# First mixing moved between the small tiles and the dense second convolution, with PSUM bank sets that swap at each step

## The reference, cut to what matters

```python
x = x + mix(x, cond, L0)      # 128x128 matrix and bias, mixed from 8 by an attention of the sample
x = x + conv(x, cond, L1)     # 9 taps over time, 4 groups of 32 channels, plus a bias of the sample
x = x + mix(x, cond, L2)
x = x + conv(x, cond, L3)
```

## Time and profile before

| | |
|---|---|
| median of 3 runs | 2650.08 us |
| the profiled execution, its own time | 2650.44 us |
| its span, first to last instruction | 2648.6 us |
| PE busy | 2627.4 us (99%) |
| PE weight loads busy | 1808.4 us (68%) |
| DVE busy | 2143.3 us (81%) |
| ACT busy | 2034.7 us (77%) |
| POOL busy | 818.0 us (31%) |
| granted TensorE clock, mean | 0.999 |

### The profile page before, as it was taken

The page is one execution under the profiler, slowest core; times in us unless marked ns, Lnnn a source line. Parts: engine busy times, 40 slices in busy tenths (PEclk is TensorE's granted clock), DMA queues, the critical chain, the costliest instruction groups (busy, mean ns, idle before and its releaser), DMA issues.

```text
span 2648.6 us, 106673 instructions
## 1 busy us (share of the span) xinstructions
PE 2627.4 (99%) x42610; PEld 1808.4 (68%) x42610; DVE 2143.3 (81%) x3093; ACT 2034.7 (77%) x3605; POOL 818.0 (31%) x1040
## 2 busy tenths in 40 slices
PE   9999999999999999999999999999999999999997
PEld 6667666766676667666766676667666766676665
DVE  8888788878887888788878887888788878887884
ACT  7777777777777777777777777777777777777774
POOL 1233233323332333233323332333233323332332
PEclk9999999999999999999999999999999999999999
DMA  4565556555655565556555655565556555655554
GB/s 166 182 205 185 180 184 195 187 180 184 196 187 180 184 195 187 180 183 196 187 180 183 194 189 180 183 195 188 180 183 195 188 180 183 195 189 180 182 176 149
DMA packets 228046, 489.82 MB, mean 185 GB/s; under 512 B 47016, under 2 KB 129072, under 8 KB 195376
## 3 DMA queue, kind: packets, MB, share of 16 engines
q1 hardware_dynamic: 228016, 489.39, 58.7%
HBM read 205.04 MB, written 150.99 MB: 134 GB/s over the span
## 4 chain that ended last, share of the span: by engine, by line
PE 98%; DVE 1%; ACT 0%; issue 0%; DVEq 0%; ACTq 0%
PE ps L361 42%; PE ps L342 28%; PE ps L313 14%; PE ps L326 13%; DVE y L680 0%; DVE y L674 0%; DVE xp L652 0%; DVE m_sum L632 0%; DVE prod L627 0%; PE ps L259 0%; DVE y_full L703 0%; PE ps L428 0%; PE ps L301 0%; PE ps L264 0%; DVE x_t L715 0%
## 5 line engine op out<-in xcount | busy, mean ns | idle before, releaser
L361 PE MATMUL ps<-y,conv_parts 32*128 32x512 f32 x18432 | 1141.7, 395 | 3.9 <-DVE y_full L703 1.8
L361 PEld LDWEIGHTS ps<-y,conv_parts 32*128 32x128 f32 x18432 | 906.5, 183 | 283.1 <-issue 131.4
L781 POOL COPY bias<-bias_table 128x4 f32 (+3 forms) x512 | 317.6, 621 | 1795.5 <-DMA o_ch<-o_ph 896.9
L680 DVE TENSOR_TENSOR y<-y_full,y 128x512 fp32r<-128x512 f32 x1020 | 636.6, 688 | 221.9 <-ACT y L497 221.9
L342 PE MATMUL ps<-y_full,conv_raw 32*32 32x512 f32 (+1 forms) x16384 | 753.8, 596 | 1.7 <-DVE y_full L703 1.7
L491 ACT ACTIVATE y_full<-ps,bias 128x512 f32<-128x512 f32 x1016 | 602.6, 707 | 26.6 <-issue 16.2
L546 ACT ACTIVATE o_ph<-ps,bias 128x512 f32<-128x512 f32 x508 | 308.5, 693 | 371.5 <-PE ps L361 371.5
L497 ACT CAST y<-y_full 128x512 fp32r<-128x512 f32 x1020 | 566.8, 663 | 0.7 <-DVE y_full L703 0.7
L342 PEld LDWEIGHTS ps<-y_full,conv_raw 32*32 32x32 f32 (+1 forms) x16384 | 275.5, 116 | 408.4 <-issue 406.2
L787 POOL COPY o_t<-o_ch 128x512 f32<-128x512 f32 x508 | 528.5, 1186 | 26.9 <-DMA o_ch<-o_ph 26.9
L491 ACT ACTIVATE y<-ps,bias 128x512 fp32r<-128x512 f32 x516 | 313.0, 690 | 191.3 <-PE ps L342 176.6
(11 more groups left out here) (60 smaller groups left out, 74.6 us busy)
## 6 DMA issues: line engine op xcount, KB each, us to landing
x_t<-x SPq DMA_DIRECT2D x128, 1024.0 KB, 5.0
o_ch<-o_ph SPq DMA_DIRECT2D x2032, 64.0 KB, 2.0
out<-o_t SPq DMA_DIRECT2D x127, 1024.0 KB, 4.0
m_parts<-mixed SPq DMA_DIRECT2D x512, 128.0 KB, 2.6
mixed<-m_own SPq DMA_DIRECT2D x128, 128.0 KB, 1.7
conv_raw<-conv_w SPq DMA_DIRECT2D x2, 768.0 KB, 9.8
mix_sb<-mix_w SPq DMA_DIRECT2D x2, 576.0 KB, 7.4
out<-x_t SPq DMA_DIRECT2D x4, 256.0 KB, 4.2
```

Source lines behind the costliest of these rows:

```text
L361: ins = nc.tensor.matmul(ps[:, bank + t, :], conv_parts[layer][rows, w, s - DENSE[0], :], src[rows, a, p_in, q:q + N], start=first, stop=f ...
L680: nc.vector.tensor_tensor(dst, full, high.bitcast(fp32), ALU.subtract).then_inc(low_set[layer], 1)
L781: nc.gpsimd.tensor_copy(bias[layer][:], bias_table[:, bass.ds(j, 1), COLUMN[layer]:COLUMN[layer] + WIDTH[layer]].rearrange("c j g -> c (j ...
```

## The change

The diff, cut to its core; left out are the bank argument that each helper now takes, the fold of the two `y1_full` buffers into one, and the written-out step 0.

```diff
+                if has(i, inner, 2):
+                    sp.wait_ge(in_time_set, 4 * (i - 1))
+                    sp.dma_start(out[i - 2], o_t[:]).then_inc(out_done, 16)
+                moves = has(i, inner, 1) and (inner or not is_last(i))
+                if moves:
+                    shuffle(i - 1, 0)
+                if has(i, inner, -1):
+                    store_matrix(i + 1)
+                if moves:
+                    for g in range(1, G):
+                        shuffle(i - 1, g)
+                if has(i, inner, -1):
+                    load_matrix(i + 1, False)
                 if has(i, inner, -3):
                     sp.wait_ge(x_low_set, 4 * (i + 2))
                     load_x(i + 3)
-                if has(i, inner, 2):
-                    sp.wait_ge(in_time_set, 4 * (i - 1))
-                    sp.dma_start(out[i - 2], o_t[:]).then_inc(out_done, 16)
-                if has(i, inner, -1):
-                    store_matrix(i + 1)
-                if has(i, inner, 1) and (inner or not is_last(i)):
-                    for g in range(G):
-                        shuffle(i - 1, g)
-                if has(i, inner, -1):
-                    load_matrix(i + 1, False)
...
-            def sparse(layer, src, begins, wait_bank):
-
-                bank = 4 if layer == 1 else 0
-                lots = WIDE + NARROW if begins else NARROW + WIDE
+            def sparse(layer, src, bank, lots):
+
...
-                        if r == 0 and begins:
-                            wait_bank(t)
                         for s, p, width in units:
                             q, p_in = divmod(s, PH)
-                            final = r == len(lots) - 1 and not begins
+                            final = layer == 1 and units is WIDE[-1]
                             if final:
                                 ins.then_inc(mm[1], 1)
...
                     q, p_in = divmod(s, PH)
+                    if k == len(order) - 1:
+                        wait_last()
                     for n, (w, a) in enumerate(PASSES):
                         first = k == 0 and n == 0 and begins
                         final = k == len(order) - 1 and n == len(PASSES) - 1 and not begins
+                own, other = own_banks(odd), other_banks(odd)
+
                 def free1(t):
-                    if not inner and i == B - 1:
-                        pe.wait_ge(full_set[2], 4 * i)
-                    elif inner or i > 0:
-                        pe.wait_ge(full_set[2], nth(i - 1, t))
+                    if inner or i > 1:
+                        pe.wait_ge(phases_set, nth(i - 2, t))
+                    elif i == 1:
+                        pe.wait_ge(full_set[0], nth(1, t))
                     elif t % 2 == 0:
                         pe.wait_ge(table_act, 2 - t // 2)
                     else:
                         pe.wait_ge(table_dve, 2 - t // 2)
 
-                def free3(t):
-                    if has(i, inner, -1):
-                        pe.wait_ge(full_set[0], nth(i + 1, t))
-                    else:
-                        pe.wait_ge(phases_set, nth(i - 2, t))
-
                 def free0(q):
                     if inner or i > 0:
-                        pe.wait_ge(phases_set, nth(i - 1, q))
+                        pe.wait_ge(low_set[1], nth(i, q))
                     else:
-                        pe.wait_ge(full_set[0], nth(1, q))
+                        pe.wait_ge(full_set[0], nth(0, q))
+
+                def free2(p):
+                    if has(i, inner, -1) and (inner or i > 0):
+                        pe.wait_ge(full_set[0], nth(i + 1, p))
+
+                def third_ready():
+                    if has(i, inner, 1):
+                        if not inner and i == 1:
+                            pe.wait_ge(conv_set, 2)
+                        pe.wait_ge(full_set[2], 4 * i)
 
                 if has(i, inner, 0):
                     if not inner and i == 0:
                         pe.wait_ge(zeros_set, 1)
                         pe.wait_ge(conv_set, 1)
                     pe.wait_ge(low_set[0], 4 * (i + 1))
-                    dense(1, y1, True, free1)
+                    dense(1, y1, own, free1, third_ready)
                     if not inner and i == 0:
                         side_bias()
                         pe.wait_ge(full_set[0], G)
-                    sparse(1, y1_full[odd], False, free1)
+                    sparse(1, y1_full, own, NARROW)
+                else:
+                    third_ready()
+                if has(i, inner, 1):
+                    sparse(3, y3_full, other, NARROW)
+                if has(i, inner, 0):
+                    sparse(1, y1_full, own, WIDE)
+                if has(i, inner, 1):
+                    sparse(3, y3_full, other, WIDE)
                 if not inner and i == 0:
                     pe.wait_ge(ctx_read, 2)
-                    first_mix(1, lambda q: pe.wait_ge(full_set[0], nth(0, q)))
+                    first_mix(1, 0, free0)
+                elif has(i, inner, -1):
+                    first_mix(i + 1, own, free0)
                 if has(i, inner, 1):
-                    if not inner and i == 1:
-                        pe.wait_ge(conv_set, 2)
-                    pe.wait_ge(full_set[2], 4 * i)
-                    sparse(3, y3_full, True, free3)
                     pe.wait_ge(low_set[2], 4 * i)
-                    dense(3, y3, False, free3)
+                    dense(3, y3, other, lambda t: None, lambda: None)
                 if has(i, inner, 0):
-                    second_mix(i)
-                if has(i, inner, -2):
-                    first_mix(i + 2, free0)
+                    second_mix(i, own, free2)
...
+                if has(i, inner, 0):
+                    high_1(i, own_banks(odd), False)
                 if has(i, inner, -1):
-                    full_0(i + 1, 1 - odd)
-                high_2(i - 1, not inner and i == 1)
+                    full_0(i + 1, own_banks(odd))
+                    high_0(i + 1)
+                output(i - 1, other_banks(odd), not inner and is_last(i), not inner and i == 1)
+                if has(i, inner, 0):
+                    full_2(i, own_banks(odd), False)
+                    high_2(i, False)
                 if has(i, inner, -2):
                     x_high(i + 2)
-                if has(i, inner, 0):
-                    high_1(i, False)
-                if has(i, inner, -1):
-                    high_0(i + 1, 1 - odd)
-                output(i - 1, not inner and is_last(i), not inner and i == 1)
-                if has(i, inner, 0):
-                    full_2(i, False)
...
+                if has(i, inner, 0):
+                    low_1(i, own_banks(odd))
                 if has(i, inner, -2):
                     matrix(0, i + 2)
+                if has(i, inner, -1):
+                    low_0(i + 1)
+                if has(i, inner, -2):
                     halves(0, i + 2)
-                low_2(i - 1)
-                if has(i, inner, -2):
-                    x_low(i + 2)
-                if has(i, inner, 0):
-                    low_1(i)
                 if has(i, inner, -1):
                     matrix(2, i + 1)
                     halves(2, i + 1)
-                    low_0(i + 1, 1 - odd)
-                if not inner and i in (B - 2, B - 1):
-                    full_2(i)
+                if has(i, inner, 0):
+                    if not inner and i == B - 1:
+                        full_2(i, own_banks(odd))
+                    low_2(i)
+                if has(i, inner, -2):
+                    x_low(i + 2)
...
-                if has(i, inner, 0) and (inner or i > 0):
-                    pool.wait_ge(full_set[2], 4 * i)
-                    set_bias(2, i)
                 if has(i, inner, 2):
                     if inner or i > 2:
                         pool.wait_ge(out_done, 16 * (i - 2))
                     for p in range(PH):
                         pool.wait_ge(shuffled[p], 16 * G * (i - 1))
-                if has(i, inner, -2):
-                    pool.wait_ge(full_set[0], 4 * (i + 2))
-                    set_bias(0, i + 2)
+                if has(i, inner, 0) and (inner or i > 0):
+                    pool.wait_ge(full_set[2], 4 * i)
+                    set_bias(2, i)
                 if has(i, inner, 2):
                     in_time(i - 2)
                 if has(i, inner, -1):
                     pool.wait_ge(low_set[1], 4 * (i + 1))
                     set_bias(1, i + 1)
+                if has(i, inner, -2):
+                    pool.wait_ge(full_set[0], 4 * (i + 2))
+                    set_bias(0, i + 2)
                 if has(i, inner, 0) and (inner or i > 0):
                     pool.wait_ge(phases_set, 4 * i)
                     set_bias(3, i)
```

(33 more changed lines are left out.)

57 lines of the change are left out of this document (34 added, 23 removed).

## The result

The changed kernel takes 2654.48 us (median of 20 runs, 2652.97 to 2657.73) against 2650.70 for the kernel before in the same series; the ratio is 1.0014, 95% interval 1.0008 to 1.0021, so it is slower by 3.8 us. The forecast was 2635.8. The profiled execution has a span of 2653.0 us where 2634.4 was worked out.

What follows compares the result with a forecast made beforehand. PE, busy for 99% of the span, was taken as the bound. Step 20.38 - 0.44 + 0.28 + 0.05 = 20.27; span 61.4 + 125 x 20.27 + 39.2 = 2634.4, time 2635.8 us, range 2594 to 2655.

Steps and rivals of the forecast that it cites:

- Bounds and seams: PE busy for 99% of the span; tile-shape seams per step fall from six to four, 1.28 to 0.84, saving 0.44 us.
- W to F: Closing from the 64-column rounds to F, a price with no row: excess taken as 0.19, between 0.13 and 0.32.
- the N rounds stand four in a row; I take 0.43: 32-column rounds on PE: the third and fourth cost 0.43 us each, W's steady round, rather than 0.45.
- both unseen prices: W to F's closing and the third and fourth N rounds; together they could shift the step by -0.06 to +0.18 us.
- D1's wait: D1's fourth product waits for ACT's output: 0.20 late plus 0.08 in the next round, +0.28 us a step, bounds 0 to 0.35.
- waking: PE starts 0.15 us after the work it waits for is ready, taken from a start at 56 us.
- F's wait: F(i+1) waits on DVE's low_1(i), nearly a tie behind W3: +0.05 us a step, between 0 and 0.2.
- a wait of 0.2 for the halves: SP's matrix store waits some 0.2 us for halves(2) between the first and second shuffle; said to cost nothing.
- Start: Written-out start: F(2) waits for low_1(1) until about 51 us; D1(2) at 61.4 us, an estimate to 2 us.
- rival D: Both waits at their upper ends, or W to F at 0.32: step 20.34 to 20.42, 2644 to 2655 us; chance 0.17.
- the likeliest case: The forecast's own case: a faster kernel, 2618 to 2645 us, chance 0.52.
- The three signs of a wrong forecast: Output ends before 2.9 after D3's last round; F starts over 2.5, or low_1 later than 1.4, after W1's last round.

Runs made afterwards that it cites:

- e2: Changed kernel, with ACT's output waiting for the bias and the four shuffles before the second convolution, not after; 2637.22 us, ratio 0.9958 to the kernel before.
- e7: Changed kernel, with SP's store of the mixed matrix behind all four shuffles instead of behind the first; 2652.19 us (one run).
- e1: Changed kernel, with the second convolution's 32-column lot put back behind the 64-column lots; 2641.88 us, ratio 0.997 to the kernel before.

## Why the prediction was wrong

- **Bounds and seams: right, but not the whole.** PE stays the bound, and F's new place gives 0.23 a step: before, F adds a closing and an opening on each side (0.13 + 0.10 + 0.09 + 0.10 = 0.42); between the small tiles and D3 it adds 0.19, its own opening 0.10 and the closing to D3 0.09, since the other two stand there anyway. M2 and D3 came out at 2.81 and 4.26 for 2.80 and 4.26. W to F, taken at 0.62, closes at 0.56, by the closer starts behind four N rounds. What is missing is a third price beside seams and new waits: PE's look-ahead ran out inside one shape.
- **The step that failed: "the N rounds stand four in a row; I take 0.43".** It was sized with the wrong question. I asked what a round costs and looked at W rounds, of which four are 64 instructions; of N rounds two are. So W's rounds at 0.43 could not tell what happens when two N lots follow, and the bounds of "-0.06 to +0.18" for both unseen prices together did not hold it: the four rounds cost 0.35 more, 0.30 with W's share, 38 us in 125 steps. The runs with 12 and 8 products and the doubled lot show why. Grouping the lots was to save one closing and one opening, 0.19 + 0.02 = 0.21; it lost 0.30.
- **D1's wait: right in kind and place, too large.** Forecast +0.28, measured 0.15 to 0.17 over a D1 without it (4.46 against 4.31 on average in e2, 4.29 in the step shown). The part that was mis-sized is waking: 0.15 was taken from a start at 56 us with PE idle; here the fourth product's weights load 0.05 after the output ends. Why waking is shorter here no run shows. The unhidden load, 0.08 forecast, is there.
- **F's wait:** forecast +0.05, measured about 0: F follows the last start of W at the usual 0.52, and takes 2.97 against 2.98.
- **SP:** forecast a wait of 0.2 for the halves in each step, measured 1 us; costing it at nothing was right inside the loop. At the end, which I took to be 39.2 us as before less a seam, the measured length is 41.8, and the chain that ends last runs through SP's shuffles. That the longer wait is the cause is argued; moving the store did not take it away (e7).
- **Start:** 61.4 forecast, 62.52 measured with a drop of the clock; without one it stood at 60.46 (e7), so 61.4 lies between the two.
- **Sum of the errors:** 125 x 0.12 for the step is 15.0 (quad +0.35, W -0.05, D1 -0.11, F -0.06), start 1.1, end 2.6: 18.7, of 2653.0 - 2634.4 = 18.6. The miss would have been larger without luck: the two waits were forecast 0.17 a step too high, 21 us in all, which hid over half of what the N rounds cost. The time lies inside the range, 2594 to 2655, at its upper edge, where the prediction had put rival D, "both waits at their upper ends"; the cause was neither of them. (That rival's own bounds, 0.07 more at D1 and 0.15 more at F, add up to a step of 20.49 and not 20.42; the range was drawn too short there.) The sign is the other one than that of the likeliest case. None of the rivals was the mechanism that decided. The three signs of a wrong forecast that the prediction named did not appear either (output ends 3.09 after D3's last round, F starts 2.28 and `low_1` 1.39 after W1's last round), since all three watched waits.

## What to carry to other kernels

When instructions of one kind are put together to save a change of tile shape, count them against PE's look-ahead: beyond 64 from the oldest unfinished one, weight loads are no longer pulled ahead, and with plain fp32 a 32x32 product is four instructions. Price a longer run from a run of that length, in instructions and not in rounds. And put waits that are long fulfilled ahead of the one that comes last: on ACT, five such waits behind it delayed its output by 0.23 us in each step (0.43 instead of 0.20 behind M2's first round), which cost time once that output became urgent.

## What the hardware showed that was not expected

- A look-ahead of 64, counted from the oldest unfinished instruction, fits all runs: 1, 5 and 9 products got ahead behind lots of 64, 48 and 32 instructions.
- Going on with the same tile shape can cost a stop like that of a change of shape: the rest of N3 starts 0.62 after N1's second round, the closing that a change costs behind an fp32 round, after one product at 0.43.
- After a wait of about 2 us on PE the granted clock was 0.51 for over 3 us in some runs (the changed kernel, e1) and stayed at 1.00 in others (e7, e2) at the same place.
- DVE's `low_0` takes 4.46 us for four parts instead of 2.50 where POOL's copies run beside it, 1.33 us instead of 0.69 for a part that falls beside a copy; DVE is busy for 88% of the span instead of 81% with the same work, at no cost to PE inside the loop.
